# Rotary self-attention: half of the query and key projections replaced by a partition shuffle on VectorE

## The reference, cut to what matters

```
def _rope(t, cos, sin):
    even = t[..., ::2]
    odd = t[..., 1::2]
    return jnp.concatenate([even * cos - odd * sin, odd * cos + even * sin], axis=-1)
q = (x @ wq.T).reshape(b, s, H, HD).transpose(0, 2, 1, 3)     # H = 16 heads of HD = 32
k = x @ wk                                                    # one key head, one value head
v = x @ wv
q = _rope(q, cos[None, None], sin[None, None])
k = _rope(k, cos[None], sin[None])
scores = jnp.einsum('bhqd,bkd->bhqk', q, k) / np.float32(np.sqrt(HD))
...                                                           # causal softmax
out = jnp.einsum('bhqk,bkd->bhqd', w, v)
return out.transpose(0, 2, 1, 3).reshape(b, s, d) @ wo.T
```

## Time and profile before

| | us |
|---|---|
| median of 3 runs | 2356.9 |
| lowest, highest run | 2355.54, 2366.66 |
| span of the profiled execution | 2357.7 |
| stage `e`: first to last instruction in the trace | about 1911.5 to 1999.8 |
| the ten projections of stage `e` (line 1363) | 1915.9 to 1950.4 |

### The profile page before, as it was taken

One profiled execution on the slowest core, in us unless ns is written; L12 is line 12 of the kernel. 1 busy time (PEld: TensorE's weight loads), 2 busy tenths in 40 slices (PEclk: granted clock), 3 DMA queues, 4 the chain that ended last, 5 costly groups with the idle time before them and its releaser, 6 DMA issues. The chain is left out here.

```text
span 2357.7 us, 26103 instructions
## 1 busy us (share of the span) xinstructions
PE 2139.3 (91%) x9842; PEld 1245.3 (53%) x9842; DVE 999.3 (42%) x2009; ACT 700.4 (30%) x1382; POOL 408.5 (17%) x468
## 2 busy tenths in 40 slices
PE   7989999999999888899999996786699977899999
PEld 3545555555555544544444442333244434799998
DVE  6455655646556404310000027999652045412120
ACT  2444544544445311321111114555302012111111
POOL 0000000000000000089989421222000000000010
PEclk9999999999999999699999998998799987799999
DMA  6102121221221404278878747443220100766652
GB/s 214 40 20 83 38 77 42 75 74 51 70 83 25 145 14 165 100 303 317 315 304 313 294 140 249 143 150 108 113 119 18 64 9 4 307 228 237 231 214 77
DMA packets 130926, 328.44 MB, mean 139 GB/s; under 512 B 39617, under 2 KB 88802, under 8 KB 111219
## 3 DMA queue, kind: packets, MB, share of 16 engines
q1 hardware_dynamic: 98368, 294.90, 34.8%
q10 hardware_dynamic: 29730, 23.29, 3.0%
q0 software_dynamic: 2704, 8.59, 1.1%
HBM read 304.71 MB, written 20.91 MB: 138 GB/s over the span
## 5 line engine op out<-in xcount | busy, mean ns | idle before, releaser
L875 PE MATMUL a_mix<-a_xn,a_probs_T 128*128 128x384 f32 (+1 forms) x832 | 315.0, 496 | 14.8 <-issue 9.9
L804 PE MATMUL a_sc<-a_wk_centred,a_ctx_T 128*128 128x512 f32 x624 | 288.1, 598 | 2.3 <-DVE a_keys L462 2.3
L875 PEld LDWEIGHTS a_mix<-a_xn,a_probs_T 128*128 128x128 f32 (+1 forms) x832 | 146.6, 192 | 122.2 <-issue 75.1
L1880 PE MATMUL c_gate_up<-bc_w_wide,c_h_rows 128*128 128x512 f32 x480 | 210.9, 592 | 0.0
L804 PEld LDWEIGHTS a_sc<-a_wk_centred,a_ctx_T 128*128 128x128 f32 x624 | 117.8, 192 | 126.2 <-issue 105.4
L1784 DVE TENSOR_TENSOR c_hidden<-c_silu,c_gate_up 128x512 f32<-128x512 f32 x38 | 26.2, 689 | 360.1 <-PE c_gate_up L1880 360.1
L1880 PEld LDWEIGHTS c_gate_up<-bc_w_wide,c_h_rows 128*128 128x128 f32 x480 | 90.1, 190 | 108.1 <-issue 108.1
L2335 PE MATMUL f_ring<-f_picked_T,f_w 128*128 128x160 f32 x1024 | 143.5, 300 | 0.0
L2350 PE MATMUL f_ring<-f_hidden,f_w 128*128 128x160 f32 x1024 | 141.4, 300 | 0.9 <-ACT f_hidden L2225 0.9
L2350 PEld LDWEIGHTS f_ring<-f_hidden,f_w 128*128 128x128 f32 x1024 | 139.3, 190 | 1.5 <-ACT f_hidden L2225 1.2
L2335 PEld LDWEIGHTS f_ring<-f_picked_T,f_w 128*128 128x128 f32 x1024 | 139.9, 190 | 0.2
(11 more groups left out here) (533 smaller groups left out, 3263.8 us busy)
## 6 DMA issues: line engine op xcount, KB each, us to landing
bc_w_wide<-in_L_ffn_W SPq DMA_DIRECT2D x64, 1024.0 KB, 5.1
f_w<-in_L_ffn_W SPq DMA_DIRECT2D x32, 2048.0 KB, 8.9
c_w_down<-in_L_ffn_W SPq DMA_DIRECT2D x34, 1024.0 KB, 7.1
a_ctx_T<-in_ctx_T SPq DMA_DIRECT2D x48, 384.0 KB, 3.5
a_xn<-in_ctx SPq DMA_DIRECT2D x24, 768.0 KB, 7.2
d_context<-in_ctx SPq DMA_DIRECT2D x8, 2304.0 KB
d_context_T<-in_ctx_T SPq DMA_DIRECT2D x12, 768.0 KB, 6.8
cd_context_T<-in_ctx_T SPq DMA_DIRECT2D x9, 768.0 KB, 7.4
```

The lines of the kernel that those rows point to most:

```text
L804: last = pe.matmul(key_bank(b, t), ctx_T[:, n % AHEAD, k, cols], wk_centred[:, k, :], start=(k == 0), stop=(k == KC - 1))
L875: ins = pe.matmul(mix[:, 0:DC], probs_T[0:m, t, p * P:(p + 1) * P], xn[0:m, b % 2, t, :], start=(t == 0), stop=(t == CT - 1))
L1880: last = pe.matmul(gate_up[2 * (u % 2) + part][:], h[:, k, :], w_wide[:, i % WIDE_RING, k, :], start=(k == 0), stop=(k == KD - 1))
```

## The change

The second set of weights goes: `L1_attn_qk` has 5 tiles of columns in place of 10, each head's even features first, and `NPROJ` is 5 with `rope` as without. For each tile VectorE makes the copy with exchanged halves itself, by a partition shuffle from the PSUM bank into `half`: within every 32 partitions (one head) partition i gets partition i+16 (mod 32). It then multiplies the bank by the cosines, multiplies `half` by the sines in place, and adds. The bank is released once, after the shuffle and the product with the cosines.

```diff
+SWAP_HALVES = list(range(16, 32)) + list(range(16))
...
-    NPROJ = NQK * (2 if rope else 1)
+    NPROJ = NQK
...
             if rope:
                 for n in range(NQK):
 
-                    u = R_PROJ + 2 * n
+                    u = R_PROJ + n
                     dve.wait_ge(ring_full, u + 1)
+                    own.did(dve.stream_shuffle(half[:], flat(ring[u % 4]), SWAP_HALVES))
                     own.did(dve.tensor_tensor(qk_T[:, n, :], flat(ring[u % 4]), cos[:], ALU.mult))
                     own.wait()
                     dve.sem_inc(ring_out, 1)
-                    dve.wait_ge(ring_full, u + 2)
-                    own.did(dve.tensor_tensor(half[:], flat(ring[(u + 1) % 4]), sin[:], ALU.mult))
+                    own.did(dve.tensor_tensor(half[:], half[:], sin[:], ALU.mult))
                     own.wait()
-                    dve.sem_inc(ring_out, 1)
                     dve.tensor_tensor(qk_T[:, n, :], qk_T[:, n, :], half[:], ALU.add).then_inc(heads_ready, 1)
                     dve.wait_ge(heads_ready, n + 1)
...
-                col = (n // 2 + n % 2 * NQK) if rope else n
                 for k in range(KD):
-                    last = pe.matmul(flat(ring[u % 4]), w[:, k, col * P:(col + 1) * P], g.hT[:, k, :],
+                    last = pe.matmul(flat(ring[u % 4]), w[:, k, n * P:(n + 1) * P], g.hT[:, k, :],
                                      start=(k == 0), stop=(k == KD - 1))
...
-        self.w = self.room[:, 0:KD * 10 * P].rearrange("p (k n) -> p k n", k=KD)
-        self.wo = self.room[:, KD * 10 * P:KD * 14 * P].rearrange("p (k n) -> p k n", k=KD)
-        self.wv = self.room[:, KD * 14 * P:KD * 14 * P + KD * 32].rearrange("p (k n) -> p k n", k=KD)
+        self.w = self.room[:, 0:KD * 5 * P].rearrange("p (k n) -> p k n", k=KD)
+        self.wo = self.room[:, KD * 5 * P:KD * 9 * P].rearrange("p (k n) -> p k n", k=KD)
+        self.wv = self.room[:, KD * 9 * P:KD * 9 * P + KD * 32].rearrange("p (k n) -> p k n", k=KD)
```

More of the change, by code:

```diff
@@ L3536, in layout @@
     even_odd = np.concatenate([np.arange(0, 32, 2), np.arange(1, 32, 2)])
-    odd_even = np.concatenate([np.arange(1, 32, 2), np.arange(0, 32, 2)])
     wq, wk = a["L1_attn_wq"].T.reshape(D, 16, 32), a["L1_attn_wk"]
-    cols = []
-    for order in (even_odd, odd_even):
-        cols += [wq[:, :, order].reshape(D, D)] + [wk[:, order]] * 4
+    cols = [wq[:, :, even_odd].reshape(D, D)] + [wk[:, even_odd]] * 4
     o["L1_attn_qk"] = lay(np.concatenate(cols, axis=1))
```

## The result

| | before | changed |
|---|---|---|
| median of the runs, us | 2358.2 (4 runs) | 2338.9 (4 runs) |
| lowest, highest | 2355.5, 2366.7 | 2336.5, 2341.3 |
| span of the profiled execution | 2357.7 | 2337.3 |

The ratio of the times is 0.991, with a 95% interval of 0.9892 to 0.9929. The time forecast was 2339.7 us. The 17.2 us of the forecast give a ratio of 0.9927.

A forecast was written before the change was run, and what follows sets the result against it. TensorE was taken to bound stage `e`; removing 40 matmul records saves 17.2 us, all else costed at nothing: 2357.7 - 17.2 = 2340.5 us of span, less 0.8 us for the median, 2339.7 us; range 2335.8 to 2345 us.

The forecast's parts named there:

- What bounds the stage: Stage `e`, projections: TensorE sets the pace, busy for all of 34.41 us, with VectorE working 8.99 us of it.
- The term of the sum: Line 1363 in stage `e`: 40 of 80 matmul records go, at 0.430 us each, a gain of 17.2 us.
- The shuffle: VectorE's loop in stage `e`: shuffle 0.69 us, set-up 0.08 us, tile 3.11 us, under TensorE's 3.44 us a tile.
- The tail: VectorE's work behind the last tile, under the value projection: `heads_ready` comes 0.3 us before it is wanted, costing nothing.
- The limit: VectorE's loop and tail in stage `e`: a shuffle of S us costs about 5 x (S - 1.01) us.
- the rival named line 1359: Stage `e`: shuffle runs as a slow permutation, eight passes of 5.5 us give 2362.2 us, TensorE waiting on `ring_out`; chance 3%.
- The weights: Fetch of query and key weights ahead of stage `e`: halved, hidden under the MLP, costed at nothing; uncovered, 3.5 us gain.
- The rival of the clock: Output projection and opening of stage `f`: later clock rise costs 4.4 us together, giving 2344.1 us; chance 7%.

The follow-up runs named there:

- `ten_projections`: The changed kernel, but TensorE computes each of the five tiles twice, VectorE shuffling the first and only releasing the second; 2359.2 us, ratio 0.9993 to the kernel before.

## Why the prediction held, step by step

**What bounds the stage.** TensorE, busy for all of the projections before and after. `ten_projections` put its work back and all of the gain went.

**The term of the sum.** 40 records at 0.430 us, 17.2 us. Stage `e` is 17.15 us shorter in the pair of profiles with early rises of the clock (90.0 and 72.9) and 17.09 us in the pair with late ones (94.0 and 76.9). That the median came within 0.8 us of the forecast is in part luck: the same kernel gave 2338.9 us in the first rounds and 2341.6 us in the second, and the spans of the first pair differ by 20.4 us.

**The shuffle.** Taken as 0.69 us, with 0.08 us of set-up. The timeline of one tile of the changed kernel:

```profile
1917.03 0.01 DVE L1215 LOAD_MASK_SELECT e_half<-e_ring  x1 [0.55 <-PE e_ring L1362]
1917.05 0.73 DVE L1215 STREAM_SHUFFLE e_half<-e_ring 128x512 f32<-128x512 f32 x1
1917.68 0.68 DVE L1216 TENSOR_TENSOR e_qk_T<-e_ring,e_cos 128x512 f32<-128x512 f32 x1
1918.50 0.69 DVE L1219 TENSOR_TENSOR e_half<-e_half,e_sin 128x512 f32<-128x512 f32 x1
1919.23 0.69 DVE L1221 TENSOR_TENSOR e_qk_T<-e_qk_T,e_half 128x512 f32<-128x512 f32 x1
1920.46 0.01 DVE L1215 LOAD_MASK_SELECT e_half<-e_ring  x1 [0.55 <-PE e_ring L1362]
```

The shuffle is 0.73 us, 0.04 more than the copy that I took for it, and its selectors load in 0.014 us. The Trainium skill, "VectorE: DVE Perf Modes", section on the perf-mode tier table, led to an estimate of 0.80 us, a little high. The loop takes 2.88 us (3.43 us from 1917.03 to 1920.46, less 0.55 us of waiting), where I had 3.11: the set-up is nearly nothing, and the product that follows the shuffle without a wait begins 0.10 us before the shuffle's record ends, where I had put a gap of 0.04 us. The wait left over is 0.55 us a tile and not 0.33. The error on the shuffle made the loop longer than forecast, the other two made it shorter by more.

**The tail.** The changed kernel's last tile:

```profile
1927.35 0.74 DVE L1215 STREAM_SHUFFLE e_half<-e_ring 128x512 f32<-128x512 f32 x1
...
1929.53 0.69 DVE L1221 TENSOR_TENSOR e_qk_T<-e_qk_T,e_half 128x512 f32<-128x512 f32 x1
...
1930.63 0.64 PE L1381 MATMUL e_bank<-e_mask_row,e_pick_row 32*64 32x512 bf16 x16
...
1931.55 0.19 DVE L1235 COPY e_v<-e_ring 128x32 f32<-128x32 f32 x1 [0.24 <-DVE e_v L1235]
...
1932.88 1.22 DVE L1246 TENSOR_REDUCE e_top<-e_bank 128x16 f32<-128x1024 f32 x1 [1.14 <-PE e_bank L1392]
```

The sum ends at 1930.22, 0.41 us before the mask (0.3 forecast; 1.9 in the earlier trace rows), and the fourth copy of values 1.1 us before the reduction. No wait stands ahead of the mask. The reduction starts 2.25 us behind the mask (2.18 in the earlier trace rows).

**The limit.** The formula, about 5 x (S - 1.01) us, came near at both points where it was tried: with six shuffles (4.6 us) it gives 18 us, and the trace shows 17.0 up to the mask; with two (1.5 us) it gives 2.4 us, and the trace shows 1.4 up to the mask. It gives too much up to the mask because the real loop is 0.23 us shorter. It leaves out the 1.3 and 0.8 us behind the mask that go with the clock, and comes out nearly right for the whole because the two errors work against each other. It also had the place wrong: the rival named line 1359, the ring under the projections, but the waits came at the values.

**The weights.** Costed at nothing, and nothing it is: the stretch ahead of stage `e` is 69.2 us with the whole fetch, with half of it and in the kernel before.

**The rival of the clock.** I gave it 7% and up to 4.4 us, 2.2 us under the output projection and 2.2 us in the opening of stage `f`, as a consequence of the new time. The kind of loss exists: a late rise costs 1.5 us in the output projection, in two profiles 3.1 us (21.7 beside 18.7). But it is no consequence of the change that any run shows, since the kernel before has it as well, and the second place was wrong. It is the start of the projections (2.0 us), for which I had costed nothing, and not the opening of stage `f`, where the records of line 2307 are as long as those of line 2308 in the earlier trace rows, 7.21 and 7.20 us (6.26 to 7.61 over all ten profiles, 7.55 and 7.53 in the second pair):

```profile
2006.22 7.21 PE L2307 MATMUL f_turned<-f_pick,hn 128*128 128x160 f32 x32 [3.51 <-DVE f_pick L2135]
```

The late rise should have been in the range as scatter of both kernels and not among the rivals. It moves single times: the changed kernel's runs go from 2336.5 to 2349.2 us over both sets, wider than the 2335.8 to 2345.0 that I gave the time.

## What to carry to other kernels

Here one engine was busy without a gap, and what moved to an idle engine was gained in full, because the other's loop stayed under the first one's pace: compute both per tile, and the distance between them is what the trade may still cost (here 0.55 us of 3.43). Past that distance the loss can be more than the delay itself: 1.4 us of delay came with 0.8 us by the clock. Look at the last tile apart, since it has only the work that follows it for cover, and ask what frees the buffer as well as what signals the result. And compare stage with stage, in more than one profile of each kernel: the two spans differed by 20.4 us, of which some 17.2 were the change.

## What the runs showed of the hardware

- A shuffle of 128 x 512 float32 from PSUM to SBUF within groups of 32 partitions took 0.72 to 0.74 us, in one instruction for all 128 partitions, with 0.014 us for its selectors, each time.
- Two operations of VectorE with no wait between them overlapped by 0.10 us in their records (the shuffle at 1917.05, 0.73 us long, and the product at 1917.68); with a wait on the engine's own semaphore between them the second began 0.04 us after the first (1939.30 after 1938.53 + 0.73, in the kernel with two shuffles).
- The granted clock rose before the first projection in some profiles and up to 4 us into the projections in others, with the same instructions of the stage ahead of it, in both kernels. The same held for the output projection (18.7, 20.1 or 21.7 us from its start to stage `f`). What decides between them was not tried.
- In the three profiles in which TensorE waited ahead of the mask (waits of 0.68 and 0.43 us in the shortest case) the granted clock was 0.52 to 0.56 from the mask to the first reduction, which took 2.98 to 3.18 us; in the changed kernel, without a wait, it was 1.00 and 2.25 us.
